# Two-layer attention on one core: the channel halves are added on GpSimd before the mean and variance products, and the second group's keys are made two tiles earlier

## The chip, the cores and the metric

The kernel runs on one core of a Trainium2 chip. TensorE (PE), VectorE (DVE), ScalarE (ACT) and GpSimd (POOL) each work through their own list of instructions and wait for one another on semaphores; SyncE (SP) issues most of the DMAs. The metric is the device time of one execution in microseconds (us); lower is better.

## The reference

Eight batches, each with 256 channels and 32x32 = 1024 positions. Layer 0 normalises each position over its channels and runs an attention with 8 heads and a position bias; layer 1 is a second attention over the result. What this case turns on is the normalisation (`k` below numbers the two halves of 128 channels that lie on the 128 partitions):

```python
mean = jnp.mean(x, axis=1, keepdims=True)
var = jnp.var(x, axis=1, keepdims=True)
xn = (x - mean) / jnp.sqrt(var + EPS) * gamma
qkv = jnp.einsum('oc,bcn->bon', w_qkv, xf)
sim = jnp.einsum('bhdi,bhdj->bhij', q, k) * scale   # + bias, softmax, times v
out = jnp.einsum('oc,bcn->bon', w_out, out) + residual
# layer 1: f, g, h projections of out; softmax(f g) over positions; gamma * (h attn) + x
```

## The kernel before, in words

**Phases.** Each batch has two groups of four heads (g = 0, 1), and each group a rows phase and a columns phase of 32 tiles. In the rows phase PE makes a 128x1024 tile of scores with two matmuls (L581, L582), DVE adds the bias and takes the row maximum (L1005), and ACT takes the exponential and the row sum (L819). Tile m + 2 of PE has to wait until DVE has read tile m, since two pairs of PSUM banks take turns, and tile m + 3 of DVE waits for ACT's tile m (three buffers). The columns phase (L602, L1019, L836, L629) makes the scores again the other way round, with the row shift already in them, and multiplies by v.

**Side work.** Everything else is put between the tiles by a table written out by hand, `side_0` for the rows phase of group 0. An entry (tile, kind, part) is done by its engine right after its own part of that tile; the order on each engine is fixed, and an engine whose next entry waits does nothing else. In the rows phase of group 0 of batch b the table holds: the second group's q (tiles 3 to 6), v (4 to 11) and k (11 to 14), each quarter of q and k being one 128x512 product (`product`, L407); the products of layer 0's output (`proj`, L472, tiles 14 to 21) and their addition to x on DVE (`add_x`, L894) for batch b - 1; `f` of layer 1 for batch b - 1 (L407 with `wfgT`, tiles 24 to 27), rounded by ACT (`high_f`, L736, tile 27) and finished by DVE (`low_f`, L903, tile 29); the row shift of the first half (`shift`, L913 to L925 on DVE, tile 18), which PE turns (L566, tile 21).

**The normalisation of batch b + 1** runs in the same phase. SP reloads `xn` with x of batch b + 1 (L381) once PE is done with v and k, behind the six DMAs that fetch q (L310). PE multiplies x by a 128x128 matrix of 1/256 to get the mean of each position, on all partitions at once: two halves of the positions times two halves of the channels, four 128x512 products at tiles 20 to 23. DVE subtracts it (`centre`, two instructions at L863, tile 23), ACT squares (L701, tile 24), PE makes the variance in the same way (four products at tiles 27 to 30), and ACT takes its logarithm (`rstd`, L710, tile 30).

```python
side_0 += [(11 + i, "k", i) for i in range(QUANTA)] + [(14, "high_k", 0), (16, "low_k", 0)]
side_0 += [(20 + i, "mean", i) for i in range(QUANTA)] + [(23, "centre", 0), (24, "square", 0)]
side_0 += [(27 + i, "var", i) for i in range(QUANTA)] + [(30, "rstd", 0)]
```

A 128x512 product of float32 stands in the trace as two MATMUL instructions. k's first quarter waits for `low_q`, DVE's last reading of the banks that q used (L872, tile 8). GpSimd sets constants at the start and does nothing after that.

## Time and profile before

| | before |
|---|---|
| median of 3 runs | 1788.33 us (1781.52 to 1788.56) |
| profiled execution: its own time, its span | 1790.26 us, 1788.5 us |
| PE busy | 1589.6 us (89%) |
| DVE busy | 1477.8 us (83%) |
| ACT busy | 1382.2 us (77%) |
| GpSimd busy | 7.1 us (0%) |
| mean granted clock of PE | 0.934 of full |

The busy shares are means over phases with different limits. Since the order on each engine is written out, the batches 1 to 6 repeat one another closely, and one of them can be read tile by tile in the timeline. All times below that look like 530.36 are microseconds from the span's start, in batch 2, whose rows phase of group 0 begins at 492.88 (DVE, tile 0) and ends at 547.86.

### The profile page before, as it was taken

Reading aid. Unit: us, or ns where it says so; the run is one execution under the profiler, and the core shown is the slowest. Engines: PE = TensorE matmul, PEld = TensorE weight load, DVE = VectorE, ACT = ScalarE, POOL = GpSimd, SP = SyncE. Lnnn points to the kernel's source line nnn. Section 1 sums busy time; section 2 is a strip of 40 time slices with the busy share of each in tenths; the row PEclk is TensorE's granted clock in tenths of the full one; section 3 lists DMA queues with packets and bytes.
Section 4 is the critical chain, followed back from the end, with each engine's and each line's share of the span. In section 5 each row is a group of like instructions: output and inputs, shape, how many; then the busy total and the mean of one; then the engine's idle time right before and its main releaser. Section 6 shows DMA issues by size and latency. Waiting matters only on the chain.

```text
span 1788.5 us, 18614 instructions
## 1 busy us (share of the span) xinstructions
PE 1589.6 (89%) x5976; PEld 753.9 (42%) x5976; DVE 1477.8 (83%) x2168; ACT 1382.2 (77%) x2033; POOL 7.1 (0%) x5
## 2 busy tenths in 40 slices
PE   6078899899998999889998999989998999999988
PEld 2043335345353544435453443535444453535424
DVE  3067988898988989898888989899889989899853
ACT  2067889788888878878787888878798887889743
POOL 1000000000000000000000000000000000000000
PEclk9577869999999999999999999999999999999999
DMA  5941204320350203501151203502043203400100
GB/s 129 248 138 36 59 1 132 93 59 1 100 148 1 60 1 107 142 25 35 48 165 37 59 1 107 142 1 60 25 124 101 60 1 90 136 1 0 39 10 23
DMA packets 57257, 122.71 MB, mean 69 GB/s; under 512 B 21428, under 2 KB 22964, under 8 KB 57160
## 3 DMA queue, kind: packets, MB, share of 16 engines
q1 hardware_dynamic: 54344, 115.37, 23.5%
q10 hardware_dynamic: 2816, 6.16, 1.3%
q8 instruction: 47, 0.77, 0.2%
q14 instruction: 50, 0.41, 0.1%
HBM read 78.92 MB, written 44.13 MB: 69 GB/s over the span
## 4 chain that ended last, share of the span: by engine, by line
PE 51%; DVE 24%; issue 18%; DMA 3%; ACT 3%; DVEq 0%; ACTq 0%; SPq 0%
DVE biased L1005 13%; PE psum L527 9%; PE psum L602 9%; PE psum L629 8%; PE psum L581 6%; PE psum L407 6%; DVE biased L1019 5%; PE psum L582 4%; PE psum L450 4%; DMA q_stack<-q_parts 2%; PE psum L460 2%; PE psum L484 1%; ACT probs L836 1%; DVE probs L931 1%; DVE x L954 1%
## 5 line engine op out<-in xcount | busy, mean ns | idle before, releaser
L1005 DVE CUSTOM_DVE_ANT_0 biased<-psum,bias_lines_sb 128x1024 f32<-128x1024 f32 x512 | 617.1, 1222 | 174.1 <-PE psum L582 163.0
L819 ACT ACTIVATE biased<-biased,nmax 128x1024 f32<-128x1024 f32 x512 | 587.4, 1148 | 162.5 <-DVE nmax L1005 157.9
L836 ACT ACTIVATE probs<-biased 128x1024 f32<-128x1024 f32 x512 | 536.8, 1057 | 128.6 <-DVE biased L1019 107.5
L1019 DVE TENSOR_TENSOR biased<-psum,bias_lines_sb 128x1024 f32<-128x1024 f32 x512 | 597.8, 1216 | 45.7 <-PE psum L602 33.4
L602 PE MATMUL psum<-q_stack,k_stack 98*128 98x512 f32 x1024 | 392.8, 490 | 38.5 <-DVE nmax L1005 15.9
L581 PE MATMUL psum<-k_stack,q_stack 96*128 96x512 f32 x512 | 331.1, 647 | 102.5 <-DMA q_stack<-q_parts 46.8
L602 PEld LDWEIGHTS psum<-q_stack,k_stack 98*128 98x128 f32 x1024 | 178.9, 200 | 328.8 <-issue 150.8
L629 PE MATMUL psum<-probs,vT 128*32 128x512 f32 x2048 | 285.1, 627 | 6.2 <-DVE st L886 3.9
L581 PEld LDWEIGHTS psum<-k_stack,q_stack 96*128 96x128 f32 x512 | 100.0, 195 | 287.1 <-DVE nmax L1005 165.8
L582 PE MATMUL psum<-k_stack,q_stack 96*128 96x512 f32 x512 | 210.8, 412 | 0.0
L527 PE MATMUL psum<-probs 128*128 128x512 f32 x384 | 186.6, 592 | 0.0
L582 PEld LDWEIGHTS psum<-k_stack,q_stack 96*128 96x128 f32 x512 | 102.7, 201 | 50.7 <-issue 47.4
L819 ACT ACTIVATION_READ_ACCUMULATOR biased<-biased,nmax 128x1 f32 x512 | 96.0, 188 | 0.0
L450 PE MATMUL psum<-xn,wqkvT 128*128 128x512 f32 x128 | 76.9, 694 | 21.4 <-DVE st L880 7.8
L527 PEld LDWEIGHTS psum<-probs 128*128 128x128 f32 x384 | 72.5, 189 | 46.0 <-issue 36.1
L629 PEld LDWEIGHTS psum<-probs,vT 128*32 128x32 f32 x2048 | 42.6, 109 | 101.3 <-issue 73.5
L761 ACT ACTIVATE probs<-probs,nmax 128x1024 f32<-128x1024 f32 x48 | 54.9, 1144 | 16.4 <-DVE probs L943 15.6
L407 PE MATMUL psum<-xn,wqkvT 128*128 128x512 f32 x128 | 66.3, 599 | 0.0
L460 PE MATMUL psum<-wqkvT,xn 128*128 128x256 f32 x256 | 65.7, 378 | 0.0
L496 PE MATMUL psum<-whT,x 128*128 128x256 f32 x256 | 65.4, 380 | 0.1
L472 PE MATMUL psum<-o,woutT 128*128 128x512 f32 x128 | 64.4, 592 | 0.8 <-ACT o L782 0.8
L527 PE MATMUL psum<-o,probs 128*128 128x512 f32 x128 | 64.8, 592 | 0.0
(78 smaller groups left out, 1090.9 us busy)
## 6 DMA issues: line engine op xcount, KB each, us to landing
q_stack<-q_parts SPq DMA_DIRECT2D x90, 256.0 KB, 5.3
k_stack<-k_parts SPq DMA_DIRECT2D x45, 512.0 KB, 7.3
q_parts<-st SPq DMA_DIRECT2D x15, 1024.0 KB, 3.9
k_parts<-st SPq DMA_DIRECT2D x15, 1024.0 KB, 4.3
xn<-in_x_dram SPq DMA_DIRECT2D x8, 1024.0 KB, 8.9
x<-in_x_dram SPq DMA_DIRECT2D x8, 1024.0 KB, 9.6
out_dram<-x SPq DMA_DIRECT2D x8, 1024.0 KB, 4.1
bias_lines_sb<-bias_lines SPq DMA_DIRECT2D x32, 240.0 KB, 15.1
```

The lines of the kernel that those rows point to most:

```text
L407: mm = pe.matmul(psum[0:rows, bank + half, :], lhsT(k), src[:, k, half * HALF:(half + 1) * HALF], start=(k == 0), stop=(k == KC - 1))
L450: mm = pe.matmul(psum[:, bank, :], wqkvT[:, k, t * C:t * C + P], xn[:, k, half * HALF:(half + 1) * HALF], start=(k == 0), stop=(k == KC - 1))
L460: mm = pe.matmul(psum[:, 4 + arg % 2, 0:C], xn[:, k, arg * P:(arg + 1) * P], wqkvT[:, k, 2 * C:3 * C], start=(k == 0), stop=(k == KC - 1))
L527: mm = pe.matmul(psum[:, 4 + 2 * c + half, :], hs[:, t % HS, c * P:(c + 1) * P], attn1[t % 3][:, half * HALF:(half + 1) * HALF], start=(t ...
L581: pe.matmul(psum[:, bank, :], lhsT, keys[:, 0:HALF], start=True, stop=True)
L582: pe.matmul(psum[:, bank + 1, :], lhsT, keys[:, HALF:N], start=True, stop=True).then_inc(SEMS["a_mm"], 1)
L602: mm = pe.matmul(psum[:, bank + i, :], k_stack[:, g, 2 * j + i, t * P:(t + 1) * P], q_stack[:, g, half, 2 * j + i, :], start=True, stop=True)
L629: mm = pe.matmul(psum[h * HD:(h + 1) * HD, 4 + half, :], vT[:, t, (g * HG + h) * HD:(g * HG + h + 1) * HD], probs[:, ((q - PV_LAG) * HP + ...
L819: nc.scalar.activation(biased[:, m % BIASED, :], biased[:, m % BIASED, :], ACT.Exp, scale=-1.0, bias=nmax[:, m:m + 1], accum_out=rowsum[:, ...
L836: nc.scalar.activation(probs[:, n % P_SLOTS], biased[:, n % BIASED, :] .rearrange("p (i n) -> p i n", i=2), ACT.Exp).then_inc(SEMS["probs_ ...
L1005: nc.vector.tensor_tensor_reduce(biased[:, m % BIASED, :], pair(bank_of(g, first, ("rows", m))), bias_lines[:, g * HG + h, a0:a0 + N], -1. ...
L1019: nc.vector.tensor_tensor(biased[:, n % BIASED, :].rearrange("p (i n) -> p i n", i=2), psum[:, bank:bank + 2, :], bias_lines[:, g * HG + 2 ...
```

## The change

GpSimd gets two additions for each batch that is made ready ahead: `sum_x` adds the two channel halves of x (waits for the load of x), `sum_squares` those of the squares (waits for both squares and for the mean's products, since both sums use one buffer, `held`). PE then needs one 128x512 product for each half of the positions, two for the mean (tiles 20, 21) and two for the variance (tiles 28, 29). `centre` and `square` move one tile forward, to 22 and 23. k's quarters move from tiles 11 to 14 to tiles 9 to 12, `high_k` and `low_k` from 14 and 16 to 12 and 14. Batch 0's own mean and variance, at the start of the program, stay as they were. To make room, `shift_rows` moves onto partitions 96 to 127 of `fg_stack`'s columns.

```diff
-        shift_rows = sb("shift_rows", [HG * NT, NHALF, P], F32R)
+        held = sb("held", [P, 2, HALF])
-        fg_stack = sb("fg_stack", [KS, 2, N], F32R)
+        fg_all = sb("fg_stack", [P, 2, N], F32R)
+        fg_stack = fg_all[0:KS]
+        shift_rows = fg_all[KS:KS + HG * NT, 0, 0:NHALF * P].rearrange("p (r n) -> p r n", n=P)
+        channel_sum = held[:].rearrange("p h n -> p (h n)")
...
-        side_0 += [(11 + i, "k", i) for i in range(QUANTA)] + [(14, "high_k", 0), (16, "low_k", 0)]
+        side_0 += [(9 + i, "k", i) for i in range(QUANTA)] + [(12, "high_k", 0), (14, "low_k", 0)]
...
-        side_0 += [(20 + i, "mean", i) for i in range(QUANTA)] + [(23, "centre", 0), (24, "square", 0)]
+        side_0 += [(17, "sum_x", 0)]
+        side_0 += [(20 + i, "mean", i) for i in range(NHALF)] + [(22, "centre", 0), (23, "square", 0)]
+        side_0 += [(24, "sum_squares", 0)]
...
-        side_0 += [(27 + i, "var", i) for i in range(QUANTA)] + [(30, "rstd", 0)]
+        side_0 += [(28 + i, "var", i) for i in range(NHALF)] + [(30, "rstd", 0)]
...
+                    if kind == "mean" and arg == 0:
+                        need(pe, "x_summed", b - 1, 1)
                         need(pe, "lo_ready", b - 1, split(1, 1))
+                    elif arg == 0:
+                        need(pe, "squares_summed", b - 1, 1)
+                    mm = pe.matmul(psum[:, 6 + arg, :], mean_w[:], channel_sum[:, arg * HALF:(arg + 1) * HALF],
+                                   start=True, stop=True)
...
+                if kind == "sum_x":
+                    need(pool, "x_loaded", b, 16)
+                    nc.gpsimd.tensor_tensor(channel_sum, xn[:, 0, :], xn[:, 1, :],
+                                            ALU.add).then_inc(SEMS["x_summed"], 1)
+                elif kind == "sum_squares":
+                    need(pool, "squared", b, KC)
+                    need(pool, "mean_mm", b, 1)
+                    nc.gpsimd.tensor_tensor(channel_sum, squares[:, 0, :], squares[:, 1, :],
+                                            ALU.add).then_inc(SEMS["squares_summed"], 1)
```

**PE, tiles 9 and 10 of the first rows phase, after the change.** L592 and L593 are the scores of a tile (L581 and L582 before), L471 is v, L413 a quarter of k.

```order
L592 MATMUL psum<-k_stack,q_stack 128x512 [waits a_max]
L593 MATMUL psum<-k_stack,q_stack 128x512
L471 MATMUL psum<-wqkvT,xn 128x256 [waits v_ready]
L471 MATMUL psum<-wqkvT,xn 128x256
L413 MATMUL psum<-xn,wqkvT 128x512 [waits lo_ready,normed]
L592 MATMUL psum<-k_stack,q_stack 128x512 [waits a_max]
L593 MATMUL psum<-k_stack,q_stack 128x512
L471 MATMUL psum<-wqkvT,xn 128x256 [waits v_ready]
```

Before, the first quarter of k with its wait for `lo_ready` stood two tiles later, behind the last of v.

**PE, tiles 20 to 22, before.** L407 with `mean_w` is a quarter of the mean, L566 the turn of the row shift.

```order
L407 MATMUL psum<-xn,mean_w 128x512 [waits lo_ready,x_loaded]
L581 MATMUL psum<-k_stack,q_stack 128x512 [waits a_max]
L582 MATMUL psum<-k_stack,q_stack 128x512
L407 MATMUL psum<-xn,mean_w 128x512
L566 MATMUL psum<-ident,shift_parts 32x128 [waits parts_ready,a_max]
L581 MATMUL psum<-k_stack,q_stack 128x512 [waits a_max]
L582 MATMUL psum<-k_stack,q_stack 128x512
L407 MATMUL psum<-xn,mean_w 128x512
```

**The same place after the change.** `held` is the buffer of GpSimd's sums.

```order
L430 MATMUL psum<-held,mean_w 128x512 [waits lo_ready,x_summed]
L592 MATMUL psum<-k_stack,q_stack 128x512 [waits a_max]
L593 MATMUL psum<-k_stack,q_stack 128x512
L430 MATMUL psum<-held,mean_w 128x512
L577 MATMUL psum<-ident,shift_parts 32x128 [waits parts_ready,a_max]
L592 MATMUL psum<-k_stack,q_stack 128x512 [waits a_max]
L593 MATMUL psum<-k_stack,q_stack 128x512
L592 MATMUL psum<-k_stack,q_stack 128x512 [waits rows_ready]
```

The first product now waits for GpSimd's sum instead of the load, and the third and fourth are gone. The variance's first product waits for `squares_summed` in the same way, after the scores of tile 28.

**GpSimd, one batch, after the change.**

```order
L868 TENSOR_TENSOR held<-xn 128x1024 [waits x_loaded]
L873 TENSOR_TENSOR held<-st 128x1024 [waits mean_mm,squared]
```

## Rows read from the trace of the kernel before

**Rows 1.** The page's busy time: us (share of the span) xinstructions.

```profile
PE 1589.6 (89%) x5976; PEld 753.9 (42%) x5976; DVE 1477.8 (83%) x2168; ACT 1382.2 (77%) x2033; POOL 7.1 (0%) x5
```

**Rows 2.** The page's chain of waits that ended last, by engine.

```profile
PE 51%; DVE 24%; issue 18%; DMA 3%; ACT 3%; DVEq 0%; ACTq 0%; SPq 0%
```

**Rows 3.** Windows: PE, PEld, DVE, ACT, POOL busy, clock, DMA, GB/s; batch 2's rows phase.

```profile
492.90:547.90 55.00, 50.36 (x170) 27.91 (x170) 47.18 (x80) 46.08 (x81) 0.00 (x0) 1.00 0.43 115
```

**Rows 4.** Timeline of PE around tiles 9 to 11: start, us, engine, line, operation.

```profile
506.94 1.03 PE L460 MATMUL psum<-wqkvT,xn 128*128 128x256 f32 x4
...
510.06 1.03 PE L460 MATMUL psum<-wqkvT,xn 128*128 128x256 f32 x4
510.92 1.02 PE L407 MATMUL psum<-xn,wqkvT 128*128 128x512 f32 x2
```

**Rows 5.** Timeline of DVE: `low_q`, behind tile 8.

```profile
507.07 1.22 DVE L872 SCALAR_TENSOR_TENSOR st<-psum,st 128x1024 fp32r<-128x1024 f32 x1
```

**Rows 6.** Timeline of DVE, from `shift` (behind tile 18) to `low_f`.

```profile
524.31 0.17 DVE L913 TENSOR_TENSOR invsum<-rowsum,invsum 128x16 f32<-128x16 f32 x1
...
525.23 0.17 DVE L925 TENSOR_TENSOR shift_parts<-shift,shift_hi 128x16 f32<-128x16 f32 x1
...
528.20 1.22 DVE L1005 CUSTOM_DVE_ANT_0 biased<-psum,bias_lines_sb 128x1024 f32<-128x1024 f32 x1
...
530.36 1.23 DVE L1005 CUSTOM_DVE_ANT_0 biased<-psum,bias_lines_sb 128x1024 f32<-128x1024 f32 x1 [0.33 <-PE psum L582]
...
532.84 2.35 DVE L863 TENSOR_TENSOR xn<-xn,psum 128x1024 f32<-128x1024 f32 x2
535.11 1.22 DVE L1005 CUSTOM_DVE_ANT_0 biased<-psum,bias_lines_sb 128x1024 f32<-128x1024 f32 x1
...
541.30 1.23 DVE L1005 CUSTOM_DVE_ANT_0 biased<-psum,bias_lines_sb 128x1024 f32<-128x1024 f32 x1 [1.48 <-PE psum L582]
...
543.94 1.28 DVE L903 SCALAR_TENSOR_TENSOR fg_stack<-psum,bfg,fg_stack 32x1024 fp32r<-32x1024 f32 x1
```

**Rows 7.** Timeline of ACT, tile 24 to `high_f`.

```profile
536.37 1.15 ACT L819 ACTIVATE biased<-biased,nmax 128x1024 f32<-128x1024 f32 x1 [2.17 <-DVE nmax L1005]
...
537.51 1.99 ACT L701 ACTIVATE st<-xn 128x1024 f32<-128x1024 f32 x2
539.41 1.13 ACT L819 ACTIVATE biased<-biased,nmax 128x1024 f32<-128x1024 f32 x1
...
542.81 1.10 ACT L736 ACTIVATE fg_stack<-psum,bfg 96x1024 fp32r<-96x1024 f32 x1
```

**Rows 8.** Timeline of SP: the fetch of q, the reload of x.

```profile
512.62 2.74 SPq L310 DMA_DIRECT2D q_stack<-q_parts  x6
516.02 0.39 SPq L381 DMA_DIRECT2D xn<-in_x_dram  x1
```

**Rows 9.** Line L381, all seven reloads of x.

```profile
DMA to landing us min/median/max: 8.5/8.9/9.6
```

**Rows 10.** Timeline of PE, tiles 20 to 22.

```profile
525.02 1.02 PE L472 MATMUL psum<-o,woutT 128*128 128x512 f32 x2
525.88 1.02 PE L407 MATMUL psum<-xn,mean_w 128*128 128x512 f32 x2
...
529.01 0.41 PE L566 MATMUL psum<-ident,shift_parts 128*32 128x128 f32 x2
529.48 0.50 PE L581 MATMUL psum<-k_stack,q_stack 96*128 96x512 f32 x1
```

**Rows 11.** Timeline of POOL: its only long instruction.

```profile
0.74 6.92 POOL L852 MEMSET k_stack<- 2x8192 f32 x1 [0.29 <-POOLq L1099]
```

**Rows 12.** Windows with the columns of rows 3: behind `centre`, the phase's end, beyond it.

```profile
533.00:536.40 3.40, 2.07 (x7) 0.72 (x5) 3.40 (x5) 1.24 (x3) 0.00 (x0) 1.00 0.88 184
...
544.80:548.20 3.40, 1.46 (x6) 0.60 (x4) 3.14 (x6) 3.05 (x7) 0.00 (x0) 1.00 0.00 0
548.20:551.60 3.40, 3.17 (x7) 1.45 (x6) 2.50 (x3) 3.34 (x7) 0.00 (x0) 0.50 0.00 0
```

More of the change, by code:

```diff
@@ L167, in two_layer_attention @@
                       rows_ready=G * NHALF, probs_ready=G * TG * HP, o_ready=G * NHALF, fg_hi=3, e1_ready=NT, hs_ready=NT)
-        for kind in (TENSOR, VECTOR, SCALAR):
+        POOL = dict(x_summed=1, squares_summed=1)
+        for kind in (TENSOR, VECTOR, SCALAR, POOL):
             for name, n in kind.items():
@@ L214, in two_layer_attention @@
                    "exp1", "invert", "scale_h", "sa", "add_y")
-        AHEAD = ("mean", "centre", "square", "var", "rstd", "norm", "q0", "high_q0", "low_q0", "k0", "high_k0",
+        AHEAD = ("sum_x", "sum_squares", "mean", "centre", "square", "var", "rstd", "norm", "q0", "high_q0", "low_q0", "k0", "high_k0",
                  "low_k0")
@@ L412, in do @@
             def do(kind, arg, b, g, first, last, tail=False):
-                if kind == "mean":
-                    if arg == 0:
-                        need(pe, "x_loaded", b, 16)
-                        need(pe, "lo_ready", b - 1, split(1, 1))
-                    product(arg, 6, lambda k: mean_w[:], xn, "mean_mm")
-                elif kind == "var":
-                    if arg == 0:
-                        need(pe, "squared", b, KC)
-                    product(arg, 6, lambda k: mean_w[:], squares, "var_mm")
+                if kind in ("mean", "var"):
+                    if b == 0:
+                        need(pe, *(("x_loaded", 0, 16) if kind == "mean" else ("squared", 0, KC)))
+                        product(arg, 6, lambda k: mean_w[:], xn if kind == "mean" else squares, kind + "_mm")
+                        return
+                    if kind == "mean" and arg == 0:
+                        need(pe, "x_summed", b - 1, 1)
+                        need(pe, "lo_ready", b - 1, split(1, 1))
+                    elif arg == 0:
+                        need(pe, "squares_summed", b - 1, 1)
+                    mm = pe.matmul(psum[:, 6 + arg, :], mean_w[:], channel_sum[:, arg * HALF:(arg + 1) * HALF],
+                                   start=True, stop=True)
+                    if arg == NHALF - 1:
+                        mm.then_inc(SEMS[kind + "_mm"], 1)
                 elif kind in ("q", "k"):
@@ L852, in _, with do, element @@
             nc.gpsimd.memset(k_stack[KS:KS + 2].bitcast(F32), 1.0).then_inc(ones_set, 1)
+            def do(kind, b):
+                if kind == "sum_x":
[7 more added lines that the diff above has]
+                                            ALU.add).then_inc(SEMS["squares_summed"], 1)
+            def element(b, first, last):
+                for n in range(A_TILES):
+                    for kind, arg, e in side_work(0, "rows", n, b, first, last):
+                        do(kind, e)
+            batches(element)
         @block.vector
```

## Prediction

> **What bounds the kernel now.** The page's busy time comes first: PE 89%, DVE 83%, ACT 77%, GpSimd next to nothing [rows 1]. The chain of waits gives PE 51%, DVE 24% and time to issue 18% [rows 2]. Both say "PE", and on that reading every product taken off PE is a gain. But both are sums over unlike stretches. The change touches one phase, the rows phase of group 0, so the windows view of that phase is next: in 55.0 us PE is busy 50.4, DVE 47.2 and ACT 46.1 [rows 3]. No engine fills it, and none is far behind; time is lost where one waits for another, and the three hand the lead to one another. So the phase has to be read in the timeline, tile by tile.
>
> Its second half has one chain on which everything hangs. Call T22 the start of DVE's tile 22, 530.36. Tile 23 and then `centre` (532.84) keep DVE until tile 24 starts at 535.11 [rows 6]. ACT takes up tile 24 at 536.37, squares from 537.51, does three tiles from 539.41 and then `high_f` from 542.81 to 543.91 [rows 7]. `low_f` on DVE starts at 543.94 [rows 6], as soon as `high_f` has ended, and tiles 30 and 31 and the phase's end stand behind it. From 536.37 on ACT has no pause in these rows. PE's own way to the same place, squares, variance products and scores between them, is as long: DVE waits 1.48 us for it before the tile at 541.30 [rows 6] and that tile and the next, 1.14 each at the least, keep it until 543.6 or later. **Two ways, ACT's and PE's, end within 0.3 us of each other.** The change shortens PE's. What it does to ACT's decides.
>
> **The change, part by part.**
>
> *Four products fewer on PE.* A 128x512 product moves PE on by 0.86 us (525.02 to 525.88) [rows 10]. Four in each of seven batches are 28 x 0.86 = 24.1 us of work. I cost the removal at nothing by itself: DVE waits for PE at T22 for 0.33 us [rows 6], and there the mean's first two products, which stay, are in front; the variance's products are covered by ACT's way above.
>
> *`centre` and `square` a tile earlier.* Before, T22 to the squares is 7.15 us (530.36 to 537.51), and the squares to `high_f` 5.30 [rows 6, 7]: 12.45. After, one DVE tile (1.14), `centre` with its hand-over to the next tile (535.11 - 532.84 = 2.27), the step from DVE's tile to ACT's (536.37 - 535.11 = 1.26) and ACT's tile (1.14) make 5.81 to the squares; but four of ACT's tiles, not three, now stand between squares and `high_f`, and one takes 1.13 (three in 539.41 to 542.81): 6.43. Together 12.24. **Gain 0.21 us for a batch**, if T22 stays.
>
> *k two tiles earlier.* Its first quarter waits for `low_q`, 507.07 to 508.29 [rows 5]. PE would be ready for it behind v of tile 9, at 506.94 + 0.86 = 507.80 (v's four instructions take 510.06 to 510.92) [rows 4]. It waits until about 508.4, 0.6 us, where before the wait had long been over. Some of that may be made good before tile 22, where DVE has slack: between 0 and 0.6, and I take 0.5, since PE then has three tiles in a row with v and k to do and DVE cannot use the time twice. `low_k` does not get longer by being moved. On SP the store of k follows, but the reload of x stands ahead of it in the list as before. The reload itself was issued at 516.02, right behind the six fetches of q, which keep SP until 512.62 + 2.74 = 515.36 [rows 8]. An earlier k can bring its issue forward by at most 0.6 us, and its data go through the queue behind q's; gain 0 to 0.6, I take 0. `shift_rows` in other partitions costs nothing that a row shows.
>
> *GpSimd's sums.* No row shows a GpSimd addition. Its one long instruction writes 8192 elements a partition in 6.92 us, 0.845 ns each [rows 11]. An addition of 1024 reads two streams and writes one. If they all run side by side it takes 0.87 us, if the two reads take turns 1.73, if all three do 2.6. I call it D and take 2.2, between the last two. The Trainium skill (GPSIMD Engine Reference, section 3.1) says that the two reads share one port and gives 4497 ns for 2048 elements; half of that is an estimate of 2.25 us, and the sum would be the same.
>
> *The wait for `sum_x`.* x lands 8.9 us (8.5 to 9.6) after its issue [rows 9], at 524.9 in batch 2. The sum runs from 525.0 to 525.0 + D, and the first product can start 0.1 later, where before it started at 525.88 [rows 10]. From that product to T22 PE needs 3.13 us to the turn (525.88 to 529.01), 0.2 for the turn and 0.88 from the scores to DVE (529.48 to 530.36) [rows 6, 10], less 0.1 that it waits in between: 4.1. So T22 = 525.1 + D + 4.1, with D = 2.2 at **531.4, 1.04 us later**. The 0.5 us of k lie beside this (530.86 without it). Behind this wait on PE stand the scores of tile 21, so DVE runs dry.
>
> *The wait for `sum_squares`.* Squares at T22 + 5.81, 1.99 long, the sum D, 0.2 for two hand-overs, a product 0.86, scores and their way to DVE 0.76, one DVE tile 1.15: T22 + 10.77 + D. ACT's way ends at T22 + 12.24 + 1.13 = T22 + 13.37. Up to D = 2.6 the wait is covered by ACT; beyond, each us of D counts twice, here and at the mean.
>
> **Sum.** For a batch 1.04 - 0.21 = 0.83 us, six times (batches 1 to 6): 5.0. Batch 7 prepares nothing and has only k's 0.5. Batch 0 has no layer 1 beside it; it loses at the mean and wins at the variance, and I take 0 (-0.5 to +1). Together +5.5 us. The profiled execution took 1790.26, so it would take 1795.8; it lies 1.9 above the median of the runs shown, and for the median I say 1788.33 + 5.5 = **1794**. With D = 0.87 only k counts, (0.5 - 0.21) x 6 + 0.5 = 2.2, 1790.5; with D = 2.6, (1.44 - 0.21) x 6 + 0.5 = 7.9, 1796. About 0.5%, or 9 us, is what a measurement of this kernel can tell from no change. This is inside it.
>
> **The rivals.**
>
> *DVE is held up beside GpSimd: slower.* DVE and GpSimd were never busy together in this phase [rows 3], so a contention between them is unknown from both sides, 0 to the whole of D. `shift` is the place: six small instructions, four of them with two inputs in SBUF, 524.31 to 525.4 before [rows 6] and 0.5 later now, 524.8 to 525.9, exactly when `sum_x` starts at 525.0. If the second of them waits until the sum ends at 527.2, tile 19 starts at 528.0 instead of 525.8. Tile 21, 528.20 + 0.5 before that, becomes 530.9, and T22 is 2.16 behind tile 21 (528.20 to 530.36) [rows 6]: 533.06, 2.7 late, 2.5 with the gain of 0.21. Six batches and k: 15.5, **1804**. It decides from the moment x lands before `shift` has ended. For it: the times fall together. Against it: L1005, which is most of DVE's work, has one input in PSUM. The Trainium skill (SBUF — State Buffer, "SBUF: two separate sides") states just this rule, an exclusive lock between a DVE instruction with two SBUF inputs and a GpSimd instruction that reads SBUF, held for the whole instruction; by it the sum would be this rival's, and no run here shows it yet. Chance 0.28.
>
> *The clock: slower.* Behind the phase's end PE's granted clock falls to half (0.50 from 548.20), after a stretch in which PE was busy 1.46 of 3.40 us; behind `centre`, with 2.07 of 3.40, it stayed at full [rows 12]. After the change tiles 22 and 23 have no products, and PE does about 1.3 in 3.4 us behind T22. If it falls there, the `f` tiles run at half speed for 3.4 us and lose up to 1.7 us of PE's work a batch, some of it on the path: up to 10 us more, 1800 to 1804. Chance 0.12.
>
> *GpSimd is slower than its streams.* At D = 3.5, T22 is 2.34 late and the squares add 0.9: 3.0 x 6 + 0.5 = 19, 1807. Chance 0.08.
>
> *The removed work counts: faster.* If ACT's way is not as firm as I read it, DVE's waits for PE go: 0.33 at T22, 1.48 at 541.30 [rows 6] and some 0.3 between, about 2.1 in seven batches, 15 us, 1773. For it speak the page's 89% and the chain; against it `low_f`, which starts 0.03 us behind `high_f`, and the wait for `sum_x`. Chance 0.10.
>
> **How the numbers follow.** My forecast 0.42, the rivals 0.28, 0.12, 0.08 and 0.10. Faster 0.10, within 0.5% 0.42, slower 0.48: likeliest is a small loss that a measurement can hardly see, but behind it stand three ways of losing more. The range 1788 to 1806 takes in D from 0.87 up, the lock and the clock, and leaves out the fast case and the slowest.
>
> **What would show it.** GpSimd's additions 1.7 to 2.6 us; PE idle about 0.8 us more before the first product on `held`; T22 about 1 us later against tile 0 of its phase, that is 38.5 where it was 37.5; `high_f` 12.2 behind T22 and `low_f` right behind it; the rows phase 55.8 where it was 55.0. The lock would show as a pause of 1 to 2 us inside `shift`; the clock as 0.5 within tiles 24 to 28. I am wrong if T22 comes earlier than before, or if `low_f` starts well before `high_f` + 1.1 would allow.

## The result, and the profile after

The changed kernel takes 1806.38 us (median of 4 runs, 1804.83 to 1808.15), the kernel before, in the same session on the same chip, 1788.07 (1781.52 to 1788.56). The medians differ by 18.3 us; the ratio, which compares the means, is 1.0111, 95% interval 1.0085 to 1.0137. The forecast was 1794 with a range up to 1806. The profiled execution took 1807.7 us, with a span of 1805.9 where it was 1788.5.

The page's busy time after, as in [rows 1]:

```profile
PE 1588.4 (88%) x5920; PEld 747.8 (41%) x5920; DVE 1489.2 (82%) x2168; ACT 1387.4 (77%) x2033; POOL 40.3 (2%) x19
```

56 MATMULs, 28 products, are gone (5976 to 5920), and yet PE is busy for the same time. DVE has exactly as many instructions as before and is busy 11.4 us longer. Both are signs to follow.

Batch 2 again, whose rows phase of group 0 now starts at 499.40 and ends at 557.47: 58.07 us where it was 54.98. Windows with the columns of [rows 3]: the whole phase, and the two stretches behind the start of `centre`.

```profile
541.80:545.20 3.40, 1.59 (x5) 0.62 (x4) 3.40 (x5) 1.24 (x3) 0.00 (x0) 1.00 0.21 40
545.20:548.60 3.40, 3.40 (x7) 1.57 (x5) 2.38 (x5) 3.40 (x7) 0.97 (x1) 0.51 0.00 0
499.40:557.50 58.10, 49.85 (x162) 26.69 (x162) 49.32 (x80) 46.33 (x81) 4.74 (x2) 0.97 0.39 110
```

In eight instructions fewer PE is busy 49.9 us (50.4 before), since from 545.20 it ran at half its clock, 0.51, in a stretch in which the kernel before kept 1.00. There the same 3.4 us behind tile 0 are:

```profile
538.68:542.08 3.40, 3.15 (x9) 1.44 (x8) 1.92 (x3) 3.40 (x6) 0.00 (x0) 1.00 0.00 0
```

DVE has its 80 instructions, as in [rows 3], and 2.1 us more of busy time.

Timeline of POOL, batch 2: the two sums.

```profile
531.89 2.35 POOL L868 TENSOR_TENSOR held<-xn 128x1024 f32<-128x1024 f32 x1 [192.26 <-DMA xn<-in_x_dram]
547.63 2.38 POOL L873 TENSOR_TENSOR held<-st 128x1024 f32<-128x1024 f32 x1 [13.38 <-ACT st L712]
```

Timeline of DVE, from `shift` to the phase's end; it answers to [rows 6].

```profile
531.58 0.17 DVE L942 TENSOR_TENSOR invsum<-rowsum,invsum 128x16 f32<-128x16 f32 x1
531.78 0.17 DVE L945 SCALAR_TENSOR_TENSOR lnsum<-invsum,lnsum 128x16 f32<-128x16 f32 x1
531.99 2.29 DVE L948 TENSOR_TENSOR shift<-nmax,lnsum 128x16 f32<-128x16 f32 x1
534.31 0.17 DVE L951 CAST shift_hi<-shift 128x16 fp32r<-128x16 f32 x1
...
539.74 1.23 DVE L1034 CUSTOM_DVE_ANT_0 biased<-psum,bias_lines_sb 128x1024 f32<-128x1024 f32 x1 [0.34 <-PE psum L593]
...
540.89 2.35 DVE L892 TENSOR_TENSOR xn<-xn,psum 128x1024 f32<-128x1024 f32 x2
...
547.68 1.22 DVE L1034 CUSTOM_DVE_ANT_0 biased<-psum,bias_lines_sb 128x1024 f32<-128x1024 f32 x1 [1.01 <-PE psum L593]
...
553.54 1.28 DVE L932 SCALAR_TENSOR_TENSOR fg_stack<-psum,bfg,fg_stack 32x1024 fp32r<-32x1024 f32 x1
...
557.47 1.23 DVE L1048 TENSOR_TENSOR biased<-psum,bias_lines_sb 128x1024 f32<-128x1024 f32 x1 [0.23 <-ACT biased L830]
```

The third instruction of `shift` handles 16 elements a partition. It took 0.17 us before, and 2.29 now: it starts 0.10 us behind GpSimd's sum and ends at 534.28, when the sum has ended (534.24). A held instruction does not stand as a wait in a profile. It looks busy, which is why DVE's busy time rose; the view to look at is the length of single instructions, against their median.

T22 (539.74) is 40.34 us behind tile 0, where it was 37.48. The 2.86 us are two things: `shift` starts at 32.18 behind tile 0, not at 31.43, 0.75 late, and its held instruction is 2.12 us too long. From T22 to the phase's end it is 17.73 us, where it was 17.50.

Timelines of PE (k's first quarter at tile 9; the mean; `f`) and of ACT (`high_f`):

```profile
514.95 1.10 PE L413 MATMUL psum<-xn,wqkvT 128*128 128x512 f32 x2 [0.47 <-DVE st L901]
...
534.30 1.13 PE L430 MATMUL psum<-held,mean_w 128*128 128x512 f32 x2 [0.98 <-POOL held L868]
535.97 0.50 PE L592 MATMUL psum<-k_stack,q_stack 96*128 96x512 f32 x1 [0.55 <-DVE nmax L1034]
...
544.43 0.50 PE L592 MATMUL psum<-k_stack,q_stack 96*128 96x512 f32 x1 [1.81 <-DVE nmax L1034]
...
545.01 1.68 PE L413 MATMUL psum<-x,wfgT 128*96 128x512 f32 x2
...
547.33 1.68 PE L413 MATMUL psum<-x,wfgT 128*96 128x512 f32 x2
```

```profile
552.04 1.10 ACT L747 ACTIVATE fg_stack<-psum,bfg 96x1024 fp32r<-96x1024 f32 x1
```

The wait, the sum and the mean look as forecast (0.98 us of wait, D 2.35), but the scores of the next tile then wait another 0.55 us for DVE, which is the later of the two.

**The other batches.** The load of x is issued at 22.45 behind tile 0 in batches 2 to 6 (23.12 before) and lands at 31.27 to 32.42. A held instruction stands in batch 0 (2.22 us) and in batches 2 to 6 (2.29, 1.56, 2.03, 1.60, 2.00 us); it is always the first that starts after the sum has. Together they are 10.7 us too long, nearly all of DVE's 11.4. In batch 1, x lands at 33.74, when `shift` is over, and none is held; there T22 is late by the landing itself: the sum starts at 33.81, 2.36 and the forecast's 4.1 behind it make 40.3, and T22 is 40.69. The rows phases of batches 0 to 7 take 59.56, 59.78, 58.07, 57.32, 57.82, 57.35, 57.78 and 52.03 us, where they took 57.60, 55.09, 54.98, 54.97, 54.97, 54.96, 54.95 and 52.89. That is 19.3 us more, against 17.4 in the span; the rest of the program gives back 1.9.

In batches 2 to 6 the phase is 2.7 us longer in the mean: 0.75 for the later `shift`, 1.7 for the hold, 0.2 behind T22. Batch 1 has no hold and still loses most, 4.7: 3.1 up to T22 and 1.6 behind it, 19.1 us from T22 to the phase's end where it was 17.5. PE's clock falls to half between 44.9 and 45.8 us behind tile 0 in every one of batches 1 to 6, where in the kernel before it fell in none of them before 55. It stays at half for 3.4 us in batches 2 to 6, and for 6.8 in batch 1, which is where that batch's 1.6 us behind T22 come from: ACT, whose pauses behind the squares are 0.35 us at most in the kernel before, waits 1.24 and 0.80 us there for DVE's tiles.

### The profile page after: what moved, and what is told of

Its sections match the earlier page's. It is cut to its first block, busy times and chain, and to the rows that moved or that the text cites. A ratio compares the mean times of both kernels' runs of the same rounds, so it can differ in the third digit from the quotient of the medians.

```text
span 1805.9 us, 18525 instructions
## 1 busy us (share of the span) xinstructions
PE 1588.4 (88%) x5920; PEld 747.8 (41%) x5920; DVE 1489.2 (82%) x2168; ACT 1387.4 (77%) x2033; POOL 40.3 (2%) x19
## 4 chain that ended last, share of the span: by engine, by line
PE 48%; DVE 26%; issue 17%; DMA 5%; ACT 4%; POOL 0%; DVEq 0%; SPq 0%; ACTq 0%
DVE biased L1034 13%; PE psum L538 9%; PE psum L613 9%; PE psum L640 7%; PE psum L592 5%; DVE biased L1048 5%; PE psum L413 4%; PE psum L593 4%; PE psum L461 4%; PE psum L471 2%; PE psum L495 2%; ACT biased L830 2%; DMA q_stack<-q_parts 2%; DMA xn<-in_x_dram 2%; PE psum L483 1%
## 5 line engine op out<-in xcount | busy, mean ns | idle before, releaser
L613 PE MATMUL psum<-q_stack,k_stack 98*128 98x512 f32 x1024 | 398.3, 497 | 38.4 <-DVE nmax L1034 17.4
L592 PE MATMUL psum<-k_stack,q_stack 96*128 96x512 f32 x512 | 327.2, 639 | 115.2 <-DVE nmax L1034 51.3
L592 PEld LDWEIGHTS psum<-k_stack,q_stack 96*128 96x128 f32 x512 | 102.0, 199 | 315.5 <-DVE nmax L1034 191.6
L593 PE MATMUL psum<-k_stack,q_stack 96*128 96x512 f32 x512 | 213.3, 417 | 0.0
L593 PEld LDWEIGHTS psum<-k_stack,q_stack 96*128 96x128 f32 x512 | 104.8, 205 | 45.7 <-issue 41.5
L413 PE MATMUL psum<-xn,wqkvT 128*128 128x512 f32 x128 | 66.9, 604 | 3.8 <-DVE st L901 3.8
L471 PE MATMUL psum<-wqkvT,xn 128*128 128x256 f32 x256 | 65.7, 378 | 0.0
```

Of the source, the lines that this page charges most:

```text
L413: mm = pe.matmul(psum[0:rows, bank + half, :], lhsT(k), src[:, k, half * HALF:(half + 1) * HALF], start=(k == 0), stop=(k == KC - 1))
L471: mm = pe.matmul(psum[:, 4 + arg % 2, 0:C], xn[:, k, arg * P:(arg + 1) * P], wqkvT[:, k, 2 * C:3 * C], start=(k == 0), stop=(k == KC - 1))
L592: pe.matmul(psum[:, bank, :], lhsT, keys[:, 0:HALF], start=True, stop=True)
L593: pe.matmul(psum[:, bank + 1, :], lhsT, keys[:, HALF:N], start=True, stop=True).then_inc(SEMS["a_mm"], 1)
L613: mm = pe.matmul(psum[:, bank + i, :], k_stack[:, g, 2 * j + i, t * P:(t + 1) * P], q_stack[:, g, half, 2 * j + i, :], start=True, stop=True)
```

## Experiments

Two theories. **The lock**: DVE is stopped whenever one of `shift`'s small instructions meets a GpSimd instruction, and that, with k's wait, is the loss. **The forecast's account**: the wait for the sum, D and k. A third runs beside them: PE's clock, which falls behind a stall. Each label has its own median, and its ratio to the kernel before in its own session.

### k alone

```diff
 (on the kernel before)
-        side_0 += [(11 + i, "k", i) for i in range(QUANTA)] + [(14, "high_k", 0), (16, "low_k", 0)]
+        side_0 += [(9 + i, "k", i) for i in range(QUANTA)] + [(12, "high_k", 0), (14, "low_k", 0)]
```

> The kernel before with k moved alone. Theory: the first quarter of k waits 0.6 us for low_q, tile 19 of each first rows phase is 0.5 to 0.8 us later against its tile 0, and the whole is 0 to 5 us slower than before (1788 to 1793). Rival: the move is a main part of the 18 us, through the DMAs or the clock, and this alone costs 6 us or more (1794 or above).

1794.50 us (1792.00 to 1797.21, 10 runs), ratio 1.0041 [1.0028, 1.0054]: 6.5 us more, where 0 to 5 were expected. PE waits as in the changed kernel:

```profile
508.53 1.10 PE L407 MATMUL psum<-xn,wqkvT 128*128 128x512 f32 x2 [0.47 <-DVE st L872]
```

T22 is 38.23 in each of batches 1 to 6, 0.75 late, and the phases 55.72 to 55.75. The wait on PE is only 0.47 us, yet T22 loses 0.75: behind the wait stand three tiles in a row with v and k. The rows phases account for 4.5 us in these six batches; where the other 2 lie is open. Alone, k's move costs a third of what the whole change does. Batch 7, which the forecast gave k's 0.5, got shorter (52.04 where it was 52.90): its T22 is 0.78 later, but a fall of the clock that the kernel before had in it at 39.0 us is missing.

### The sums alone

```diff
 (on the changed kernel)
-        side_0 += [(9 + i, "k", i) for i in range(QUANTA)] + [(12, "high_k", 0), (14, "low_k", 0)]
+        side_0 += [(11 + i, "k", i) for i in range(QUANTA)] + [(14, "high_k", 0), (16, "low_k", 0)]
```

> The changed kernel with k back at tiles 11 to 14: the sums alone. Theory (stall beside GpSimd, then PE waits): shift now runs from 31.4 to 32.5 against tile 0, x lands at about 32.1, so only its last instructions can be held; T22 38.8 to 40.5, and 8 to 14 us slower than before: 1796 to 1802. Rival (k's move is most of it): under 1792.

1804.87 us (1800.24 to 1806.91), ratio 1.0093 [1.0074, 1.0112]: 18.8 above the kernel before of its own session, where the changed kernel was 18.3 above its own. By the ratios k's move adds some 3 us to the sums, by the medians nothing; alone it costs 6.5. With k in its old place `shift` starts at 31.42 and x lands at 31.21 to 32.14, so now all of batches 1 to 6 meet, each for 2.25 to 2.36 us; T22 is 39.54 to 39.65. In batch 3 the sum ends at 33.75 behind tile 0 and T22 is 39.65; in the changed kernel 33.71 and 39.61. Where the same instruction is held, the end of the sum sets T22, and an earlier or later start of `shift` is hidden behind it: so the two edits do not add up. In batch 1 the instruction held is a CAST, with one input:

```profile
320.38 2.35 DVE L951 CAST shift_hi<-shift 128x16 fp32r<-128x16 f32 x1
```

### A sum that nobody needs

The products of the kernel before, k early, `shift_rows` where the changed kernel has it, and GpSimd adding the halves of x into a buffer that nothing reads. `centre` waits for it only so that x is not overwritten under it.

```diff
 (on "k alone")
+        side_0 += [(17, "sum_x", 0)]
...
+                    need(dve, "x_summed", b - 1, 1)
```

> The kernel of e1_k_only, and GpSimd adds the halves of x into a buffer that nobody reads; PE makes four products as before and waits for the load alone. Lock theory: in the batches whose x lands before shift has ended (five of seven), one instruction of shift takes about 2.3 us instead of 0.17, and the time is 5 to 10 us above e1_k_only. Rival (the loss is PE waiting for the sums): shift takes its 1.0 us, the time is within 2 us of e1_k_only.

1808.99 us (1805.63 to 1811.31), ratio 1.0119 [1.0095, 1.0143]: 14.5 us above "k alone", more than the 5 to 10 expected. No product waits for GpSimd here and PE has all its work, so this is **the price of the meeting itself**, with the falls of the clock that follow it. Timeline of POOL, then of DVE, batch 3:

```profile
735.61 2.36 POOL L862 TENSOR_TENSOR held<-xn 128x1024 f32<-128x1024 f32 x1 [205.70 <-DMA xn<-in_x_dram]
```

```profile
735.57 0.17 DVE L940 SCALAR_TENSOR_TENSOR lnsum<-invsum,lnsum 128x16 f32<-128x16 f32 x1
735.78 2.22 DVE L943 TENSOR_TENSOR shift<-nmax,lnsum 128x16 f32<-128x16 f32 x1
738.03 0.17 DVE L946 CAST shift_hi<-shift 128x16 fp32r<-128x16 f32 x1
```

The one that starts before the sum runs free, the next is held to the sum's end. Batch 1, where x lands at 33.76, behind `shift`, has no hold, T22 at 38.26 and a phase of 55.75, as in "k alone": the sum costs nothing where the two do not meet. In batches 2, 4 and 6 T22 is 40.2 to 40.4, that is 38.23 and the hold. In batches 3 and 5 it is 41.62 and 42.11: there PE's clock fell to half at 38 us, behind the stall, and T22 is 1.3 and 1.7 us later than the hold explains. Between 40 and 50 us, where it fell in the changed kernel, the clock fell in no batch here.

### A memset in place of the sum

```diff
 (on "a sum that nobody needs")
-                    nc.gpsimd.tensor_tensor(channel_sum, xn[:, 0, :], xn[:, 1, :],
-                                            ALU.add).then_inc(SEMS["x_summed"], 1)
+                    nc.gpsimd.memset(channel_sum, 0.0).then_inc(SEMS["x_summed"], 1)
```

> The kernel of e4_unused_sum with GpSimd only writing the 128x1024 buffer in place of adding into it, so it reads nothing from SBUF. If only a GpSimd instruction that reads SBUF holds DVE up: shift keeps its 0.17 us instructions, time as e1_k_only, 1792 to 1797. If any GpSimd work does: one instruction of shift takes up to 0.9 us in the batches where the two meet, a few us above e1_k_only.

1798.11 us (1793.87 to 1800.14, 3 runs), ratio 1.0054 [1.0028, 1.0079]; the interval overlaps that of "k alone", so the time decides nothing and the rows must. Timeline of POOL, batches 3 and 4, then of DVE in the same two places:

```profile
729.73 0.97 POOL L862 MEMSET held<- 128x1024 f32 x1 [205.72 <-DMA xn<-in_x_dram]
935.41 0.95 POOL L862 MEMSET held<- 128x1024 f32 x1 [204.71 <-DMA xn<-in_x_dram]
```

```profile
729.64 0.17 DVE L945 CAST shift_hi<-shift 128x16 fp32r<-128x16 f32 x1
729.84 0.88 DVE L947 COPY shift_parts<-shift_hi 128x16 f32<-128x16 f32 x1
...
935.45 0.17 DVE L939 SCALAR_TENSOR_TENSOR lnsum<-invsum,lnsum 128x16 f32<-128x16 f32 x1
935.66 0.17 DVE L942 TENSOR_TENSOR shift<-nmax,lnsum 128x16 f32<-128x16 f32 x1
935.87 0.52 DVE L945 CAST shift_hi<-shift 128x16 fp32r<-128x16 f32 x1
```

Both at 935.45 and 935.66 have two inputs and run free beside the memset, which reads nothing; the CAST and the COPY, with one, are held to its end (936.36, and 730.70). Batch 5 shows the same, 0.17 for two two-input forms and 0.37 for the CAST. The last instruction of `shift`, which has two inputs again, starts 0.09 us behind the COPY in every trace and cannot be read apart from it. Beside the sum, which reads, every kind was held. The Trainium skill (SBUF — State Buffer, "SBUF: two separate sides") says that a DVE operation with two SBUF inputs meets only a GpSimd operation that reads SBUF, while one in a 2-port performance mode meets any. The runs agree with both halves, if CAST and COPY are taken to be of the second kind, which no row says.

### `shift` one tile earlier

```diff
 (on the changed kernel)
-        for side, at in ((side_0, HM), (side_1, HM + 2)):
-            side += [(at, "ln", 0), (at + 2, "shift", 0), (at + 5, "turn", 0), (at + 4, "keep_rows", 0)]
+        for side, at, by in ((side_0, HM, 1), (side_1, HM + 2, 2)):
+            side += [(at, "ln", 0), (at + by, "shift", 0), (at + 5, "turn", 0), (at + 4, "keep_rows", 0)]
```

> The changed kernel with shift one tile earlier (tile 17), so that it ends before x lands; all else is left. Lock theory: no instruction of shift over 0.2 us, T22 at about 38.8 against tile 0 instead of 40.3, time 7 to 10 us below the changed kernel: 1796 to 1799. Rival: PE's wait for the sum takes the place of the stall, T22 stays near 40, time above 1803.

1821.26 us (1818.01 to 1823.98), ratio 1.0188 [1.0163, 1.0214]: slower, where 1796 to 1799 was expected. `shift` starts at 31.1, and x now lands at 31.08 to 31.74 in batches 3 to 6, so they meet still. The stall sits where PE has least to do. Windows of batch 3 (columns of [rows 3]), the stall and what follows:

```profile
741.20:744.60 3.40, 0.31 (x2) 0.28 (x2) 3.30 (x8) 0.30 (x1) 1.18 (x1) 0.99 0.38 135
744.60:748.00 3.40, 3.40 (x7) 1.65 (x6) 2.55 (x5) 2.90 (x5) 0.00 (x0) 0.50 1.06 219
```

PE was busy 0.31 of 3.40 us, then ran at half its clock; T22 is 42.9, the phase 60.2. In batch 2, without a meeting, 39.25 and 56.56.

**Three unused products at tiles 22 to 24** on top of this, to keep PE busy:

> e3_shift_17 and, on PE, three 128x512 products of weights that nobody reads, behind tiles 22, 23 and 24, where PE would stand still. They leave the result as it is. Clock theory: no fall of the granted clock within tiles 24 to 28, and 4 to 8 us less than e3_shift_17, though PE does 2.6 us more work a batch. Rival (the fall is covered by ACT's way to high_f): same time as e3_shift_17 within 2 us.

1817.00 us (1812.74 to 1822.78), ratio 1.0167 [1.0138, 1.0197]. Meetings in batches 4 to 6 gave T22 42.9 again; the fall of the clock at 44.4 us that batch 1 had is gone. But in batch 3, met above, nothing was held here, so the difference to the run above is not the products' alone, and nothing follows from it for the time. Batch 1 does tell something: no instruction was held in it in either run, and from T22 to the phase's end it took 18.84 us with the fall of 6.8 us and 17.31 without. A fall of that length costs 1.5 us there.

### `shift` at tile 20, `turn` at 22

```diff
 (on the changed kernel)
-        for side, at in ((side_0, HM), (side_1, HM + 2)):
-            side += [(at, "ln", 0), (at + 2, "shift", 0), (at + 5, "turn", 0), (at + 4, "keep_rows", 0)]
+        for side, at, by, turn, keep in ((side_0, HM, 4, 6, 5), (side_1, HM + 2, 2, 5, 4)):
+            side += [(at, "ln", 0), (at + by, "shift", 0), (at + turn, "turn", 0), (at + keep, "keep_rows", 0)]
```

> The changed kernel with shift at tile 20, where sum_x has ended, turn at 22, keep_rows at 21. Theory: no instruction of shift over 0.2 us in any batch, T22 at 38.2 to 38.9 against tile 0 (x landing + 0.1 + 2.37 + 0.15 + about 4) instead of 39.6 to 40.3, and 7 to 12 us below the changed kernel: 1794 to 1799. Rival (a stall moved is not a stall removed): DVE is held elsewhere beside GpSimd, or T22 stays over 39.3, and the time is above 1802.

1799.31 us (1799.14 to 1799.82), ratio 1.0070 [1.0055, 1.0085], 7 us below the changed kernel. `shift` (35.07) comes behind the sum, and batches 2 to 6 have no hold. **Here the forecast's own mechanism can be seen alone**: T22 = start of the sum + D + 4.1. In batches 2, 5 and 6 the sum starts at 32.44, 31.51 and 32.04; with D = 2.37 that gives 38.91, 37.98 and 38.51, and T22 was 38.80, 37.87 and 38.40, each 0.11 earlier: 4.0 in place of 4.1. Batches 3 and 4 (31.34 and 31.29) fit the formula too, with T22 at 37.81, but test nothing, since batch 7, which has no sum, has 37.81 as well. Batch 1 (x lands at 33.83, a hold of 1.21 us, a fall of the clock at 36.7) took 59.17 us, the others 55.1 to 56.1.

### Taking sum and `shift` apart at tile 17

k back at 11 to 14, `shift` at 17, the mean's products at 21 and 22:

```diff
 (on "shift one tile earlier")
-        side_0 += [(9 + i, "k", i) for i in range(QUANTA)] + [(12, "high_k", 0), (14, "low_k", 0)]
+        side_0 += [(11 + i, "k", i) for i in range(QUANTA)] + [(14, "high_k", 0), (16, "low_k", 0)]
...
-        side_0 += [(20 + i, "mean", i) for i in range(NHALF)] + [(22, "centre", 0), (23, "square", 0)]
+        side_0 += [(21 + i, "mean", i) for i in range(NHALF)] + [(22, "centre", 0), (23, "square", 0)]
```

> The sums with every wait hidden: k back at 11 to 14, shift at tile 17 (ends at 31.4, before x lands), the mean's two products at tiles 21 and 22, centre 22, square 23. Theory: no stall in shift, no wait of PE for sum_x, T22 at 37.4 to 37.7 as before, low_f still right behind high_f, so the four products saved gain nothing or 0.2 us a batch: 1785 to 1791. Rival (PE's work counts once the waits are gone): 10 us or more below the kernel before, under 1779.

1797.17 us (1785.63 to 1799.26, 10 runs), ratio 1.0057 [1.0040, 1.0074]. The profiled execution is the fastest of them and shows what was meant, T22 37.49 to 37.53, phases 54.79 to 55.22, in batches 1 to 6 but for batch 4, where x landed at 31.04 and met the last instruction of `shift` (31.19): 2.32 us held, T22 41.95, a phase of 59.51. The ten runs spread over 14 us, and only one was profiled. That the longer ones had more such meetings would fit. So would falls of the clock without any meeting: the mean granted clock was 0.932 in the fastest and 0.927 to 0.930 in the nine others, and the next run has 0.927 to 0.928 at the same times.

**The same with `sum_x` also waiting for the end of `shift`**, so that they cannot meet:

```diff
 (on "taking sum and `shift` apart")
                 if kind == "sum_x":
                     need(pool, "x_loaded", b, 16)
+                    need(pool, "parts_ready", b - 1, 1)
```

> e8_apart, and sum_x on GpSimd also waits for shift, so that the two can never meet, wherever x lands. If the hold beside GpSimd is all that made e8_apart slow and uneven (1785.6 to 1799.3): no held instruction in any batch, all runs within some 5 us, 1778 to 1786, which is 2 to 9 us below the kernel before. Rival: the unevenness is the clock's or the DMAs', and the runs still spread over 10 us, with a median above 1790.

1798.30 us (1796.59 to 1801.70), ratio 1.0065 [1.0053, 1.0078]. No instruction is held and the spread is down to 5 us, but no time is won; 1778 to 1786 was expected. In batches 2 to 6 PE's clock falls to half at 32.6 us, just behind `shift`. Windows, batch 2:

```profile
522.90:526.30 3.40, 1.65 (x6) 0.68 (x5) 3.26 (x12) 1.27 (x3) 0.45 (x1) 1.00 1.02 414
526.30:529.70 3.40, 3.40 (x6) 2.04 (x7) 2.82 (x5) 2.90 (x5) 1.91 (x1) 0.52 0.26 80
```

T22 is 39.11 and the phase 56.4; in batch 1, which kept its clock there, 37.51 and 54.82. The price of one such fall is 1.6 us.

**The kernel before with `shift` at 17**, to see whether that place has a price of its own:

> The kernel before with shift at tile 17 and nothing else, to see what of e9_behind_shift comes from that alone. Expected: DVE's work is the same, T22 at 37.5 as before, time within 3 us of before: 1784 to 1790. If shift's place is the gain, 1783 or less.

1796.83 us (1793.48 to 1797.26), ratio 1.0051 [1.0037, 1.0065]. It has, 9.8 us where at most 3 were expected: T22 38.37, the phase 55.84 to 55.86 instead of 54.97, and 57.49 where the clock fell at 32.6. It is not the place alone: the two runs above have `shift` there too, with the mean at 21 and 22, and T22 at 37.5 wherever the clock held. But with the falls at 32.6 tile 17 was the wrong place for the test, and the sum had to move instead.

**`f` one tile earlier** on the version with the extra wait (`f` 23 to 26, `high_f` 26, `low_f` 28), to see whether `high_f`'s place in ACT's row is the end:

> e9_behind_shift with f, high_f and low_f a tile earlier (23 to 26, 26, 28): high_f has three of ACT's tiles, not four, between itself and the squares. If ACT's way to high_f sets the end of the phase, as the prediction said, the phase gets up to 1.1 us shorter in six batches, 3 to 6 us below e9_behind_shift. Rival: ACT's own work or the variance's wait ends as late, and the time is the same within 2 us.

1794.71 us (1792.88 to 1795.73), ratio 1.0045 [1.0030, 1.0061]. Batches 1, 4 and 5, which kept their clock at 32 us, took 54.81, 54.82 and 55.13, no less than in the run without it (54.82, batch 1), though `high_f` now starts 11.11 us behind T22 instead of 12.25. Moving `f` shortened nothing. In both runs ACT pauses once between the squares and the phase's end, for 0.35 us, as it did in the kernel before: it is the amount of ACT's work that sets the end, and not the place of `high_f` in it. The 3.6 us won would fit the number of falls at 32.6 in the two profiles, four in batches 2 to 7 instead of six.

### The sum behind `shift`, which stays at 18

```diff
 (on the changed kernel)
-        side_0 += [(9 + i, "k", i) for i in range(QUANTA)] + [(12, "high_k", 0), (14, "low_k", 0)]
+        side_0 += [(11 + i, "k", i) for i in range(QUANTA)] + [(14, "high_k", 0), (16, "low_k", 0)]
...
-        side_0 += [(20 + i, "mean", i) for i in range(NHALF)] + [(22, "centre", 0), (23, "square", 0)]
+        side_0 += [(21 + i, "mean", i) for i in range(NHALF)] + [(22, "centre", 0), (23, "square", 0)]
...
                     need(pool, "x_loaded", b, 16)
+                    need(pool, "parts_ready", b - 1, 1)
```

> The changed kernel with k back at tiles 11 to 14, shift left at tile 18, the mean's products at 21 and 22, and sum_x held back until shift has ended. The add then runs from about 32.7 to 35.1 us behind tile 0, and the first product at tile 21 (turn and scores of tile 22 behind it, at 36.6 in the kernel before) is not late. Theory (all that the change costs is the held shift, k's wait and the fall of the clock that follows a stall): no instruction of shift over 0.3 us, T22 37.5 to 37.7, rows phases 54.7 to 54.9, and a time of 1783 to 1788, that is the kernel before less about 1 us. Rival 1 (the clock): PE has less to do around tiles 20 to 28 and its clock falls to half in most batches at 32 to 36 or 44 to 46 us, phases 55.2 to 56.8, 1790 to 1800. Rival 2 (DVE and GpSimd also collide outside shift): instructions of DVE other than those of shift are longer beside the add.

**1786.87 us** (1780.38 to 1790.64, 12 runs), ratio 0.9996 [0.9982, 1.0009]: the kernel before, to within 0.2%. T22 is 37.47 to 37.49 in batches 1 to 6, no instruction of `shift` is over 0.2 us. Timeline of GpSimd and DVE, batch 2: beside the sum, DVE's tiles and `add_x`, which have one input in PSUM, keep their usual lengths.

```profile
523.53 2.37 POOL L869 TENSOR_TENSOR held<-xn 128x1024 f32<-128x1024 f32 x1 [191.02 <-DVE shift_parts L955]
```

```profile
524.45 0.68 DVE L924 TENSOR_TENSOR x<-x,psum 128x512 f32<-128x512 f32 x1
525.05 1.22 DVE L1035 CUSTOM_DVE_ANT_0 biased<-psum,bias_lines_sb 128x1024 f32<-128x1024 f32 x1
```

The whole loss is gone with the meeting, the wait and k's move, so the sums and the missing products cost nothing of their own. Nor do they win anything. Windows: batch 2 behind the start of `centre`, then its whole phase, then that of batch 6.

```profile
529.80:533.20 3.40, 1.58 (x5) 0.61 (x6) 3.40 (x5) 1.24 (x3) 0.00 (x0) 1.00 1.03 214
533.20:536.60 3.40, 3.40 (x7) 1.84 (x8) 2.17 (x4) 3.40 (x5) 0.36 (x1) 0.52 0.17 33
490.88:546.06 55.18, 49.14 (x162) 26.91 (x162) 47.28 (x80) 46.15 (x81) 4.74 (x2) 0.97 0.42 115
1314.57:1369.34 54.77, 47.75 (x162) 26.06 (x162) 47.07 (x80) 46.13 (x81) 4.74 (x2) 1.00 0.42 116
```

In batches 3 and 6, which keep the clock, the phase is 54.8, 0.2 below before. In batches 1, 2, 4 and 5 it falls to half at 42 to 44 us, behind a stretch in which PE had 1.58 of 3.40 us to do, and the phase is 55.2, 0.2 above before. Work taken off PE was partly paid back by a slower PE. This fall goes with the missing products: in the five profiled kernels that keep all of PE's products (before, k alone, the unused sum, the memset, before with `shift` at 17) the clock fell between 40 and 50 us in none of batches 1 to 6; it did in six in the changed kernel and with the sums alone, in four here and in three in the next run. They are not enough for it: with `shift` at tile 20, where they are missing too, it fell there in none.

**The same with k at 9 to 12:**

> The same with k at tiles 9 to 12, that is the changed kernel with two edits only: sum_x waits for shift, the mean's products one tile later. Theory (k's wait costs what it did alone, no more): shift 0.75 later, T22 38.2 to 38.3, no held instruction, rows phases 55.5 to 55.7, and a time 5 to 7 us above the run with k at 11 to 14 in the same call, about 1790 to 1794. Rival (a PE that is late and has little to do lets its clock fall at 44 to 46 us in most batches, as in the changed kernel): 1795 to 1802.

1797.53 us (1794.41 to 1798.38, 5 runs), ratio 1.0057 [1.0042, 1.0072]. This is the changed kernel with two edits, the wait and the mean a tile later: 8.9 us of its loss are gone. T22 is 38.22 to 38.25 in batches 2 to 6, phases 55.5 to 55.9 (batch 1, where x lands at 33.98: 38.73 and 56.4). It stands 10.7 us above the run before it, more than the 5 to 7 expected: rows phases hold 6.5 of the two spans' 10.4, and 3.0 lie before the first tile, which starts at 100.5 instead of 97.5. Over all profiled executions that start lies between 95.5 and 100.5 with no edit that explains it, so the spans of two single profiles can differ by 5 us for that alone. In steps of these medians the loss is: sums put apart -0.4, k early +10.7, sum and `shift` left to meet (with the mean at 20) +8.9; the last step compares two sessions, and by the ratios it is about 9.6. Another order gives other steps: on the kernel before, k costs 6.5 and the meeting on top of it 14.5.

## Why the prediction was wrong

Its sign was right, and its forecast was too small by 12.4 us. Two terms that it put at or near nothing make most of the difference: the hold of `shift`, and k's move.

- **The removed products at nothing: right.** With everything else put right, 24.1 us of PE's work less moved the time by -0.4 us (by the interval, -3.2 to +1.6). Its reason was right in the main: ACT's work sets the phase's end where the clock holds. The way through `high_f` was not, since `high_f` a tile earlier changed nothing. The page's 89%, and the chain that gave PE half of the span, were no argument.
- **`centre` a tile earlier, -0.21: right, and then eaten.** T22 to the phase's end was 17.30 (54.77 - 37.47) where the clock held, 17.50 before: -0.20. T22 to `high_f` is 12.30, forecast 12.24. With the fall at 44 to 46 it is 17.73.
- **D = 2.2: right** (2.34 to 2.40 in all sums), and so was T22 = sum + D + 4.1, as the run with `shift` at tile 20 shows within 0.11 us. But in the changed kernel the later of the two waits at T22 is the one for DVE. The estimate of 2.25 worked out from the Trainium skill (GPSIMD Engine Reference, section 3.1) is 0.1 short of the measured 2.37.
- **The contention of DVE beside GpSimd, taken at 0: the step that failed.** It was given 0.28 as a rival, with the right instruction, and "about 2.7 us late" for T22 was 2.86. The forecast set against it that DVE's long instruction has one input in PSUM. True, and beside the point: six instructions of 0.17 us are enough, since one of them, met once, stops DVE for 2 us. The two times stood in the prediction, `shift` at 524.8 to 525.9 and the sum from 525.0; with them the rival should have been the forecast. What the runs show in place of the 0: a hold of 1.4 to 2.1 us in batch 0 and in batches 2 to 6, worth 8.9 us between the last run above and the changed kernel, and 14.5 on top of "k alone". That the rival's 1804 comes near 1806.38 is partly luck: batch 1, which it gave 2.5 us like the others, had no hold and lost 4.7, and batch 0, put at 0 (-0.5 to +1), lost 2.0.
- **k's 0.5, and hidden behind the wait for the sum: too small, the second step that failed.** At T22 it is 0.75, above the end of 0.6 that the wait was given. The wait was 0.47 us; what it does to T22 is more than its length, and the run with k alone shows that without explaining the last 0.3 us. In the sum k stood only with batch 7's 0.5; measured, the move costs 6.5 us alone and 10.7 with the sums put apart. Even without a meeting the forecast comes out too small: the last run has T22 at 38.2 and phases of 55.5 to 55.9 in batches 2 to 6, near the forecast's 38.5 and 55.8, and is 10.3 us above the kernel before, not 5.5. In its profile batch 1 lost 1.3 and batch 0 0.9, and 2.0 stand before the first tile; how much of this is k's is open.
- **Gain of k at the landing, 0: not decided.** The issue came 0.67 us earlier, the landing at 31.27 to 32.42 (31.95 to 32.28 before). But the runs with k at 11 to 14 have landings from 31.04 on too, so an earlier landing is no mark of k. Where `shift` and the sum were left free to meet, an early landing was no gain: it brought the sum into `shift`.
- **The clock as a rival, 0.12: it came true beside the lock.** It fell where the prediction put it, at the `f` tiles, in six batches of six, and for its reason as far as the runs tell: it came only where the products are missing, and there without a meeting too (four of six batches with the sum behind `shift`), while the unused sum met `shift` and had none there. A fall of 3.4 us costs 0.4 us a batch (55.18 against 54.77); one of 6.8 us, in batch 1, costs the 1.5 to 1.6 that the prediction allowed with "up to 1.7". Elsewhere it is dear: 1.3 to 1.7 us at 32 to 38 us, where PE is the late one. Rivals that can hold together should not have been given separate chances only.

Still open: what moves the landing of x between executions (batch 1's at 33.74 made its T22 late), why an early k costs more than the rows phases account for, and why the clock falls in some batches and not in others that look the same.

## What to carry to other kernels

Before moving work to GpSimd, list what DVE does in that stretch, the smallest instructions first, and ask of each whether all its operands are in SBUF; one short instruction that starts beside a long GpSimd one waits for the rest of it, and if it feeds other engines they wait too. Put the GpSimd instruction behind such a group with an explicit wait, and its reader one tile later: the two together were worth 9 us here, and with k in its old place they brought the kernel back to the time before. They were not tried apart. Taking work off the engine with the highest share gives nothing where it only waits longer; check in the windows whether its clock falls afterwards.

## What the runs showed of the hardware

A 128x1024 float32 addition of two SBUF operands on GpSimd takes 2.34 to 2.40 us, a memset of the same size 0.95 to 0.97. A DVE instruction of 0.17 us with all its operands in SBUF that starts while the addition runs ends with it, stands as busy in the records and takes up to 2.36 us there; one with an input in PSUM keeps its 0.68 or 1.22 us. Not expected was that beside a memset the two-input forms run free and the one-input CAST and COPY are held. Nor was it that a stall of 2 us on DVE can cost more than its length: in two of the five batches of the unused sum that had a hold behind batch 0, PE's granted clock fell to half behind it, and T22 was 1.3 and 1.7 us later than the hold explains. A fall of 3.4 us cost 1.6 us at 32.6 and 0.4 at 42 to 46, one of 6.8 us 1.5 at 44.
